# Attention normalised along features by way of DRAM, with the projections and the feed-forward moved between rests

## The reference

```python
logits = einsum('bihd,bjhd->bhij', q, k) * scale + SLOPES * rel      # causal mask: -inf
attn = softmax(logits)
x = layernorm(x + einsum('bhij,bjhd->bihd', attn, v) @ Wout)
h = silu(x @ wg.T) * (x @ wu.T)          # wg, wu, wd: integers times 1/127
x = layernorm(x + h @ wd.T)
```

## Time and profile before

| what | value |
|---|---|
| median of 3 runs | 2138.42 us (2137.84 to 2139.09) |
| profiled execution | 2136.29 us, of which the span from first to last instruction is 2134.6 us |
| TensorE busy | 1983.0 us, 93% |
| VectorE | 1595.1 us, 75% |
| ScalarE | 1223.5 us, 57% |
| GpSimd | 928.5 us, 43% |
| mean granted clock of TensorE | 0.981 |
| DMA | 229.09 MB, 48.5% of 16 engines' span |

### The profile page before, as it was taken

One profiled execution on the slowest core, in us unless ns is written; L12 is line 12 of the kernel. 1 busy time (PEld: TensorE's weight loads), 2 busy tenths in 40 slices (PEclk: granted clock), 3 DMA queues, 4 the chain that ended last, 5 costly groups with the idle time before them and its releaser, 6 DMA issues.

```text
span 2134.6 us, 47883 instructions
## 1 busy us (share of the span) xinstructions
PE 1983.0 (93%) x19236; PEld 1550.0 (73%) x19236; DVE 1595.1 (75%) x2765; ACT 1223.5 (57%) x1999; POOL 928.5 (43%) x1924
## 2 busy tenths in 40 slices
PE   4779999999999999999999999999999999999986
PEld 3557777777777777777777777777877877777766
DVE  4557777787777787777778777778777778777754
ACT  1446656555655656655655665565565665566552
POOL 0123444444444453444454444444344445444444
PEclk8789999999999999999999999999999999999998
DMA  7455455355555445545545545545554544553500
GB/s 205 103 120 105 101 112 118 96 112 114 115 112 110 103 108 106 128 103 108 113 100 112 121 109 111 116 97 114 106 122 109 106 109 102 111 125 91 100 16 21
DMA packets 148830, 229.09 MB, mean 107 GB/s; under 512 B 13552, under 2 KB 64496, under 8 KB 148592
## 3 DMA queue, kind: packets, MB, share of 16 engines
q1 hardware_dynamic: 148608, 226.02, 48.5%
HBM read 139.98 MB, written 84.93 MB: 105 GB/s over the span
## 4 chain that ended last, share of the span: by engine, by line
PE 80%; DVE 10%; ACT 5%; DMA 2%; issue 1%; SPq 1%; POOL 0%; POOLq 0%; DVEq 0%
PE pair L495 72%; PE pair L498 8%; DVE row_max L801 7%; ACT probs L726 3%; DVE staged_lo L786 2%; ACT staged_hi L704 2%; DMA q_rows<-max_lo 1%; SPq L471 0%; DMA q_rows<-bounce 0%; DMA probs<-L_attn_Wout 0%; SPq L480 0%; DMA bounce<-staged_lo 0%; DVE row_max L803 0%; DVE xt_lo L786 0%; DVE x1t_lo L786 0%
## 5 line engine op out<-in xcount | busy, mean ns | idle before, releaser
L726 ACT ACTIVATE probs<-pair 128x1024 f32<-128x1024 f32 x640 | 627.1, 1027 | 150.1 <-PE pair L495 149.8
L903 POOL TENSOR_SCALAR_AFFINE_SELECT probs<-probs 128x256 f32<-128x256 f32 (+1 forms) x896 | 371.5, 440 | 445.9 <-ACT probs L726 445.1
L910 POOL TENSOR_TENSOR h_lo<-h_full,h_hi 128x256 fp32r<-128x256 f32 x384 | 283.2, 738 | 507.6 <-ACT h_hi L751 496.9
L803 DVE TENSOR_REDUCE row_max<-pair 128x8 f32<-128x1024 f32 x256 | 312.6, 1221 | 115.2 <-PE pair L495 114.7
L801 DVE TENSOR_REDUCE row_max<-pair 128x2 f32<-128x1024 f32 x256 | 311.9, 1218 | 71.2 <-PE pair L495 71.2
L495 PE MATMUL pair<-q_rows,k_rows 64*128 64x512 f32 (+3 forms) x2048 | 321.0, 370 | 38.4 <-DMA q_rows<-max_lo 20.8
L495 PE MATMUL pair<-k_rows,q_rows 52*128 52x512 f32 (+3 forms) x2048 | 299.6, 351 | 60.2 <-DVE staged_lo L786 26.1
L495 PE MATMUL pair<-probs,v_ones 128*32 128x512 f32 (+3 forms) x4096 | 319.3, 441 | 0.8 <-ACT probs L726 0.8
L495 PEld LDWEIGHTS pair<-q_rows,k_rows 64*128 64x128 f32 x2048 | 167.8, 188 | 157.2 <-ACT probs L726 92.2
L495 PEld LDWEIGHTS pair<-k_rows,q_rows 52*128 52x128 f32 x2048 | 179.0, 190 | 122.9 <-DVE row_max L801 62.9
L704 ACT ACTIVATE staged_hi<-pair 128x512 fp32r<-128x512 f32 x128 | 76.6, 599 | 269.9 <-PE pair L495 260.5
(11 more groups left out here) (88 smaller groups left out, 3622.7 us busy)
## 6 DMA issues: line engine op xcount, KB each, us to landing
bounce<-staged_hi SPq DMA_DIRECT2D x128, 256.0 KB
bounce<-staged_lo SPq DMA_DIRECT2D x128, 256.0 KB
q_rows<-bounce SPq DMA_DIRECT2D x128, 256.0 KB, 5.2
k_rows<-bounce SPq DMA_DIRECT2D x128, 256.0 KB, 6.2
x_sb<-L_attn_x SPq DMA_DIRECT2D x32, 512.0 KB, 10.4
k_rows<-bounce SPq DMA_DIRECT2D x128, 128.0 KB, 5.5
q_rows<-bounce SPq DMA_DIRECT2D x128, 128.0 KB, 6.7
x<-L_attn_x SPq DMA_DIRECT2D x32, 512.0 KB, 9.1
```

The lines of the kernel that those rows point to most:

```text
L726: scalar.activation(probs[g][:, tile, :, :], pair[:, :, :], ACT.Exp, scale=scale).then_inc(s_exp, 1)
L803: vector.tensor_reduce(maxima[:, QB2_PARTS:QB0 + 1, :, p].rearrange("p b s -> p s b"), pair[:, :, :].rearrange("p s (b n) -> p s b n", n=P ...
L903: made = pool.affine_select(out=diagonal, in_=diagonal, compare_op=ALU.is_ge, fill=0.0, base=0, pattern=[[0, diagonal.shape[1]], [1, P]], ...
L910: pool.tensor_tensor(h_lo[:, m, :], h_full[(n_split_h[step] - 1) % H_BUFFERS][:, :], h_hi[:, m, :].bitcast(F32), ALU.subtract).then_inc(s_ ...
```

## The change

Attention is normalised with features on partitions, and no transposes are needed for it. `send` writes pv_t to DRAM (one DMA), `fetch` reads back the 64 rows of sums into `attn` and one denominator row per head into `sums`, laid over 128 partitions of 16 elements (two DMAs), `recip` takes the reciprocals on VectorE, `send_recip` writes them to DRAM, and `fetch_recip` reads each head's row back 16 times, into `recips`. This is done per unit and group of 4 heads, 5 DMAs each. Once per unit GpSimd multiplies (`divide`), ScalarE makes attn_hi and GpSimd subtracts for attn_lo. The steps `turn`, `divide` on VectorE and the transposes "attn" are gone.

The order of the rests is new as well: `divide`, `attn_hi` and `attn_lo` of unit w-3 stand at the head of each rest; the output projection is in the even rest, the value projection at the end of the odd rest, one sequence ahead; the transposes of x1 are in the odd rest; the feed-forward's halves run one rest later, so that the list has one more `w`; and norm1, which stood behind `down` and in the next attention part, stands between the gate_up tiles of the even rest.

```diff
-        for w in range(-2, self.units + 4):
+        for w in range(-2, self.units + 5):
...
                     self.add("pv_copy", u, g)
+                    self.add("send", u, g)
+                    if g == 1:
+                        self.add("fetch", u, g)
...
     def rest(self, w):
-        k = w // 2
-        ffn, part = k - 2, w % 2
+        k, part = w // 2, 1 - w % 2
+        ffn = k - 2 - part
         has_ffn = 0 <= ffn < self.batches
         if self.has(w + 1):
             self.add("gather", w + 1)
...
+        if self.has(w - 3):
+            self.add("divide", w - 3)
+            self.add("attn_hi", w - 3)
+            self.add("attn_lo", w - 3)
+        if w % 2 == 1:
+            self.project(w + 2, 0)
+            if w == -1:
+                self.ffn_weights()
             if has_ffn:
                 self.transposed("x1", ffn)
...
+        if has_ffn:
+            self.gate_up(ffn, part, range(0, 2))
+        self.max_row(w)
+        if self.has(w - 2):
+            self.add("recip", w - 2, 1)
+            self.add("send_recip", w - 2, 1)
+        if self.has(w - 1):
+            self.add("fetch", w - 1, 0)
+        if w % 2 == 1 and 0 <= k - 1 < self.batches:
+            self.add("load_residual", k - 1)
+        if has_ffn:
+            self.gate_up(ffn, part, range(2, 3))
+        if w % 2 == 0 and 0 <= k - 2 < self.batches:
+            self.project_out(k - 2, 0)
+            self.project_out(k - 2, 2)
+        if has_ffn:
+            self.gate_up(ffn, part, range(3, 4))
+        if w % 2 == 0 and 0 <= k - 2 < self.batches:
+            self.add("norm1", k - 2, 0)
+        if w % 2 == 0 and 0 <= k + 1 < self.batches:
+            self.transposed("x", k + 1)
+            if k + 2 < self.batches:
+                self.add("load_x", k + 2)
+        if has_ffn:
+            self.gate_up(ffn, part, range(4, 6))
+        if w % 2 == 0 and 0 <= k - 2 < self.batches:
+            self.add("norm1", k - 2, 2)
+        if self.has(w - 2):
+            self.add("fetch_recip", w - 2, 1)
+        if self.has(w - 1):
+            self.add("recip", w - 1, 0)
+            self.add("send_recip", w - 1, 0)
+        if w % 2 == 0:
+            self.project(w + 2, 0)
+        if has_ffn:
+            self.down(ffn, part)
+        self.project(w + 2, 1)
+        if w % 2 == 1 and 0 <= k + 1 < self.batches:
+            self.values(k + 1, 0)
+            self.values(k + 1, 2)
+        if self.has(w - 1):
+            self.add("fetch_recip", w - 1, 0)
...
+                elif kind == "attn_hi":
+                    u, = key
+                    e.wait_ge(s_divide, n_divide["divide", u])
+                    if u >= 2:
+                        e.wait_ge(s_work, n_work["out", u // 2 - 1, 2])
+                    scalar.activation(attn_hi[:, u % 2, :], attn[u % 2][:, :], ACT.Copy).then_inc(s_attn_hi, 1)
...
+                elif kind == "recip":
+                    u, g = key
+                    z = u % 2
+                    e.wait_ge(s_fetched[z][g], (u // 2 + 1) * 16 * 2)
+                    if u >= 2:
+                        e.wait_ge(s_recip_sent[z][g], (u // 2) * 16)
+                    vector.reciprocal(small_recips[z][:, g, :], sums[z][:, g, :]).then_inc(s_recip, 1)
...
+                elif kind == "divide":
+                    u, = key
+                    z = u % 2
+                    for g in range(2):
+                        e.wait_ge(s_fetched[z][g], (u // 2 + 1) * 16 * 2)
+                        e.wait_ge(s_recip_fetched[z][g], (u // 2 + 1) * 16)
+                    pool.tensor_tensor(attn[z][:, :], attn[z][:, :], recips[z][:, :], ALU.mult).then_inc(s_divide, 1)
...
+                elif kind == "attn_lo":
+                    u, = key
+                    e.wait_ge(s_attn_hi, n_attn_hi["attn_hi", u])
+                    pool.tensor_tensor(attn_lo[:, u % 2, :], attn[u % 2][:, :], attn_hi[:, u % 2, :].bitcast(F32),
+                                       ALU.subtract).then_inc(s_attn_lo, 1)
```

158 lines of the change are left out of this document (56 added, 102 removed).

## The result

The changed kernel takes **2459.8 us** (median of 4 runs, 2449.9 to 2469.5) against 2138.1 us for the kernel before on the same chip: ratio 1.151, 95% interval 1.144 to 1.157, 322 us slower. The forecast was 2377 us; the time lies inside the range, at its far end. The profiled execution's span is 2449.1 us.

A forecast was written before the change was run, and what follows sets the result against it. The prediction took TensorE to bound the kernel, most tightly in the rests. Its terms, -2.6 + 3.9 + 2.1 + 2.5 - 0.3 + 1.7, gave +7.3 us per period, 234 over 32, plus 5 for the tail: 2377 us, range 2215 to 2470.

The forecast's parts named there:

- wait for x1t_lo, odd rest: Odd rest: TensorE's gate_up waits for x1t_lo, queued behind the division and attn_hi; 3.9 us per period (3.5 to 4.1).
- wait for attn_lo, even rest: Even rest: the output projection waits for attn_lo of the division made in the same rest; 2.1 us (1.7 to 2.4).
- wait for h_lo: Even rest: TensorE's down projection waits for h_lo, with norm1 between the h_lo on GpSimd; 2.5 us (0 to 3).
- last reciprocal and start of attention: Rest's end and first row_max: late reciprocal fetch against a 0.45 us stall that may go; -0.3 us per period taken.
- clock: TensorE's granted clock falls after a long wait: one fall per period counted, 1.7 us; ends 0 and three falls, 5.1.
- with 3.5 it is there at 18.3: Odd rest: with a 3.5 us landing, the last reciprocal's fetch arrives at 18.3 us; VectorE stands from 13.9.
- issued by 11.3, needed at 14.7: 0 to 3: Even rest: the last reciprocal's fetch is issued by 11.3 us and needed at 14.7, costing 0 to 3 us.
- Since few other transfers run then: Last reciprocal's fetch: few other transfers then, so landing near a lone 256 KB store's, at the -0.3 us end.
- 28 at 0.62 us are 17 us of 31, not a bound: SP's queue: 28 DMA issues per unit at 0.62 us take 17 of 31 us, so SP doesn't bound.
- The tail: End of the kernel: one more rest, with the last unit's round trips over DRAM bare; +5 us.
- The rival of 14.2 us per period: Whole period: every wait costs a clock fall and the late reciprocal holds VectorE; 454 us more, 2597 us; 8% above 2470.
- the attention part itself would grow: Attention parts: forecast still near 14.5 us; growth would mean the DRAM trips bound them and the argument is wrong.

The follow-up runs named there:

- e2: The change with division, attn_hi and attn_lo of unit w-3 moved from the head of the rest into the attention part before it; 2431.5 us.
- e8: e5 with norm1 behind the down projection and, in the odd rest, x1's transposes ahead of the projection and the row maxima's ahead of gate_up; 2321.3 us.
- e5: The change with division, attn_hi and attn_lo in the attention part and the last reciprocal behind the last projection; 2367.5 us.
- e9: e8 with SP's queue reordered so no landing wait stands ahead of anything, a third attn buffer, and the division back in the rest; 2352.2 us.
- e11: e9 with the fetches behind the stores of the row maxima, and the division ahead of gate_up's first tile; 2283.9 us.
- e12: e11 with the reciprocals in the next attention part and, in odd rests, the fetches and residual-input load behind gate_up tile 3; 2145.5 us.
- e3: The change with norm1 put back behind the down projection, its second half behind a select of the next attention part; 2482.9 us.

## Why the prediction was right, and where it was off

**Direction, place and two of the three waits' sizes** were right. Per period, forecast against measured:

| term | forecast | measured |
|---|---|---|
| wait for x1t_lo, odd rest | 3.9 | 3.8 |
| wait for attn_lo, even rest | 2.1 | 1.9 |
| wait for h_lo | 2.5 | 1.6 |
| last reciprocal and start of attention | -0.3 | -0.4 behind the odd rest, +1.4 behind the even one |
| wait for xt_lo | not in the sum | +0.6 |
| clock | 1.7 | 3.6, of which 0.65 is also in the +1.4 |

The division's two operations took 1.27 us each where 1.4 was taken between bounds of 1.06 and 1.48 from the earlier trace rows; the argument from the order of each engine's queue, with prices of single instructions from the trace, gave the first two waits to 0.2 us and the third 0.9 too high. That the three waits can go by moving steps and that they then are worth so little alone (28 us for e2) was not in it.

**The clock** was the largest miss, 1.9 us per period or 61 us. The step that failed is "I count one per period". One and more is what the odd rest alone brings: it fell in each of 22, and for twice as long in 6 of them. To these come the even rests, 9 of 22, and 8 attention parts. The upper bound of three falls, 5.1, held. By the Trainium skill (TensorE: Matmul & The Clock Gate, "HAM oscillation") a recurring wait costs a fall each time; the trace agrees for the wait of 3.8 us and disagrees for that of 1.9. Its reading, 5.1 us of clock, would have been 1.5 too high where the forecast was 1.9 too low.

**The reciprocal in the even rest** was the second, some 1.4 us per period. In the odd rest the forecast was near: "with 3.5 it is there at 18.3", behind VectorE's 13.9, is 4.4 us of standing, and in the period shown VectorE stood 4.92 us and went on 4.8 us after the issue (1171.42 to 1176.24); the attention part behind it became 0.4 us shorter, as forecast. The step that failed is the sentence on the even rest, "issued by 11.3, needed at 14.7: 0 to 3", of which the sum took 0. There VectorE went on 9.0 us after the issue, more than the 2.2 to 6.7 of the earlier trace rows, stood 5.28 us, and the attention part behind it grew from 14.5 to 15.9 us. "Since few other transfers run then" was wrong there: over the stretches from 1124 to 1130 the DMA share was 1.04 and 1.06, and the gather was still on its way. The fixed cost by the Trainium skill (DMA: Bandwidth & Descriptors, "Anatomy of one DMA"), 2.3 us as an estimate, is that of a transfer by itself, fitted on GpSimd's path, while these are issued by SP; here the measurement is four times that.

**"28 at 0.62 us are 17 us of 31, not a bound"** counted only the issues. SP's queue also stands at the landings: 306.5 us in the change for pv_bounce and 241.7 for recip_bounce, and 846 in e8. In e5 to e8 the chain and TensorE's wait for the row maxima point at that queue; that the standing itself was their limit isn't shown, since e9 took most of it away and was no faster.

**The tail** was put at +5 us for one more rest; from the last combine to the end it is 25 us longer.

The rival of 14.2 us per period named both things at their full price and got 8%; the truth, 9.8, lies between it and the forecast. That the attention part itself would grow was named as what would make the argument wrong, with the DRAM trips as its cause. It did in part: of 44 attention parts between 400 and 2000 us, 31 took 14.0 to 14.7 us (14.5 before) and 13 took 15.0 to 19.7, all of them behind an even rest. The argument from TensorE's rests holds for most of the time, and the trips, with the falls they cost, are the part that it missed. The time lies inside the range by 10 us of its 255; the clock, the reciprocal, xt_lo and the tail came out larger than forecast and the three waits smaller, so that margin is no merit of the sum.

**What stays open**: the split of e11's 68 us and of e12's 138 us between their two moves each, what the queue's order is worth on top of e8, and the split of e3's loss between clock and staged_lo. The clock not granted is an upper bound of its cost, since some of it falls on idle time, so more than 0.4 us of the period may be unexplained.

## What to carry to other kernels

A round trip to DRAM on an engine's in-order path must be priced as issue, queue in front and landing under load, here up to 9 us and not 3.5, and its consumer belongs a whole stage later. The slowdown was in the order of the steps: the same work and transfers took 2460 us in one order and 2146 in another (with a third buffer for `attn`), with every wait for a landing and every small urgent store placed deliberately in the one queue, and the division, the output projection, norm1 and x1's transposes moved too. What the removed transposes should have given, 84 us, it still didn't gain. And when a wait is removed and the time hardly moves, look at what grew in its place: in e2 the rests gave 5.7 us per period and the attention parts took 5.4 back. And look again after each step: the theory of two loops had the direction for e5 (28 and 47 us singly, 92 together), but its times for e5 to e8 were 96 to 246 us too low, while TensorE's wait for the row maxima grew from 20 us in the change to 133 in e8.

## What the runs showed of the hardware that was not expected

- Issuing a DMA is not always short: in e9 one 8 KB store held SP's queue for 4.03 us (DMA share 1.05 and 1.13) and in e11 a load for 4.29 (share 1.06 and then 0.54); in the kernel before no single issue between 300 and 2040 us took over 2.1 us, and in the change none over 1.6. The share doesn't tell them apart: the change had shares of 1.04 and 1.06 with issues of 0.6 us. What does is not shown.
- The landing of a small transfer took longer here with a gather just in front: the store of the reciprocals (8 KB) let SP go on 8.9 us after its issue in the even rest of the change (1129.54 to 1138.47), where the gather's last issue was 3 us before it, and 4.2 us after it in the odd rest (1170.32 to 1174.51), where that was 7 us before. In e9 the last of the four stores of the row maxima (8 KB each) was issued 8.7 us before TensorE, which waits for all four, went on.
- The same wait can bring the clock down or not: behind the wait of 1.86 us for attn_lo the granted clock was 0.63 in the next 3 us in one even rest and 1.00 in the next one; it fell in 9 of 22. Behind the wait of 3.8 us it fell in 22 of 22.
- GpSimd's float32 product and subtraction with two inputs of 128x512 took 1.27 us, 1.7 times the 0.74 us of half the size.
